# First and last two iterations with their own orders, weights prepared on GpSimd, fusion products in other banks, filler matmuls

## What is computed

```python
q, k, v = (silu(causal_conv4(xn @ W)) for W in (Wq, Wk, Wv))
beta = sigmoid(xn @ Wb)
# delta rule over time; its triangular system is inverted per block
delta = delta_rule(l2norm(q), l2norm(k), v * beta, beta)
# depthwise convolutions of 3, 15 and 31 taps on v, then two products
ms = channel_mixer(kernel_mix(concat(conv3(v), conv15(v), conv31(v))))
feat = concat(xn, mean|ms|, mean|delta|, mean|v|)      # 512 + 12 columns
w = softmax(gelu(feat @ w1 + b1) @ w2 + b2)            # 3 weights per head
o = w0 * ms + w1 * delta + w2 * v
att = (o * rsqrt(mean(o * o)) * o_norm_w) @ Wo
# ffn: mixing of each token with the one before it
ffn = sigmoid(xr @ Wr.T) * ((relu(xk @ Wk.T) ** 2) @ Wv.T)
out = x + att + ffn
```

## Time and profile before

| | us |
|---|---|
| median of 3 runs | 3527.82 (3523.88 to 3529.14) |
| the profiled execution | 3519.07 |
| its span, first to last instruction | 3517.3 |
| TensorE busy | 3315.3 (94%) |
| VectorE busy | 3165.9 (90%) |
| ScalarE busy | 2758.2 (78%) |
| GpSimd busy | 807.7 (23%) |

### The profile page before, as it was taken

The page is one execution under the profiler, slowest core; times in us unless marked ns, Lnnn a source line. Parts: engine busy times, 40 slices in busy tenths (PEclk is TensorE's granted clock), DMA queues, the critical chain, the costliest instruction groups (busy, mean ns, idle before and its releaser), DMA issues.

```text
span 3517.3 us, 69963 instructions
## 1 busy us (share of the span) xinstructions
PE 3315.3 (94%) x22848; PEld 2447.8 (70%) x22848; DVE 3165.9 (90%) x7856; ACT 2758.2 (78%) x9144; POOL 807.7 (23%) x1489
## 2 busy tenths in 40 slices
PE   6899999999999999999999999999999999999986
PEld 5677777667777667776677776777766677767754
DVE  6999998999999999989999999999899899989993
ACT  5677888778887778787778887778877788877774
POOL 2022221122221222221222211222212222112220
PEclk8999999999999999999999999999999999999998
DMA  6022221122211122211222111222111222112220
GB/s 183 11 50 51 50 40 33 29 51 51 50 32 33 37 51 51 50 28 25 49 51 51 36 38 29 50 51 50 32 33 38 51 50 43 35 24 51 45 44 7
DMA packets 188307, 154.92 MB, mean 44 GB/s; under 512 B 111804, under 2 KB 146108, under 8 KB 187688
## 3 DMA queue, kind: packets, MB, share of 16 engines
q0 software_dynamic: 31744, 79.70, 13.1%
q1 hardware_dynamic: 156200, 70.76, 7.7%
HBM read 51.34 MB, written 52.95 MB: 30 GB/s over the span
## 4 chain that ended last, share of the span: by engine, by line
PE 35%; DVE 25%; ACT 21%; issue 9%; DMA 7%; POOL 2%; ACTq 0%; DVEq 0%; POOLq 0%; SPq 0%
DVE my L1531 19%; PE dense L721 6%; DMA my<-prod 5%; PE dense L674 5%; PE dense L678 5%; PE dense L662 3%; ACT my L1106 3%; PE small L690 2%; ACT dense L1136 2%; PE cell L644 2%; PE cell L645 2%; PE cell L637 2%; ACT kT L926 1%; DMA rows_out<-Bm 1%; ACT xsh L856 1%
## 5 line engine op out<-in xcount | busy, mean ns | idle before, releaser
L1531 DVE SCALAR_TENSOR_TENSOR my<-vT,mw,my 128x256 f32<-128x256 f32 x5408 | 2245.4, 480 | 38.9 <-DMA my<-prod 24.3
L721 PE MATMUL dense<-xsh,w 128*128 128x256 f32 x2048 | 483.2, 382 | 3.9
L397 POOL TENSOR_SCALAR vare<-xsq 128x2 f32<-128x2 f32 x32 | 6.2, 194 | 2081.8 <-ACT xsh L856 2081.8
L721 PEld LDWEIGHTS dense<-xsh,w 128*128 128x128 f32 x2048 | 369.4, 190 | 72.3 <-ACT xr L1168 11.1
L1079 ACT ACTIVATE ka<-dense 128x512 f32<-128x512 f32 x64 | 38.2, 597 | 319.3 <-PE dense L662 319.3
L662 PE MATMUL dense<-xk,wfk 128*128 128x256 f32 x1024 | 250.1, 400 | 22.0 <-DVE xb L1591 16.8
L662 PEld LDWEIGHTS dense<-xk,wfk 128*128 128x128 f32 x1024 | 198.4, 199 | 74.9 <-issue 47.0
L674 PE MATMUL dense<-wr,xr 128*128 128x512 f32 x512 | 235.4, 603 | 0.0
L516 PE MATMUL front<-xsh,wq 128*128 128x256 f32 x1024 | 231.9, 379 | 0.0
L678 PE MATMUL dense<-wfv,ka 128*128 128x512 f32 x512 | 230.2, 592 | 0.0
L516 PE MATMUL front<-xsh,wv 128*128 128x256 f32 x1024 | 228.7, 381 | 0.8 <-ACT xsh L871 0.8
(11 more groups left out here) (182 smaller groups left out, 6803.2 us busy)
## 6 DMA issues: line engine op xcount, KB each, us to landing
my<-prod POOLq DMA_DIRECT2D x160, 384.0 KB, 4.2
xa<-in_x SPq DMA_DIRECT2D x32, 512.0 KB, 4.2
rows_out<-Bm SPq DMA_DIRECT2D x64, 256.0 KB, 4.3
out<-xb POOLq DMA_DIRECT2D x32, 512.0 KB, 14.7
Yq<-units_out SPq DMA_DIRECT2D x128, 32.0 KB, 2.1
w<-in_w SPq DMA_DIRECT2D x1, 2048.0 KB, 17.2
Bu<-rows_out SPq DMA_DIRECT2D x32, 64.0 KB, 2.9
units_out<-Xu SPq DMA_DIRECT2D x32, 64.0 KB, 2.5
```

The source lines that it names most:

```text
L721: e.matmul(by_batch(o), w1[:, k, hs(2 * pair + c)], xsh[s % 2][:, k, :, 1:1 + P], start=(k == 0), stop=False)
L1531: i = e.scalar_tensor_tensor(o, vT[s % 2][:, c, :, off:off + P], mw[:, col:col + 1], o, ALU.mult, ALU.add)
```

## The change

(a) The loop runs over `range(2, NS)` only; what the first two and the last two iterations did is written out, with an order of its own on TensorE, ScalarE, VectorE and GpSimd. In the first two, ScalarE sums and squares x of step 1 right after x of step 0, GpSimd takes `deviation(1)` early and `norms_k(0)` and `norms_q(0)` last, and ScalarE copies and starts convolving each projected pair as it comes. In the last two, `ffn_out` of the last step moves ahead of the joining of the block inverse, `state` behind the logits, and `scale_B`, `copy_beta` and others take other places. (b) `prepare_weights` moves from VectorE to GpSimd, behind the inversion of step 0, in 12 instead of 15 instructions: a part is now taken away from the rows below it by a mask that is 1 from row 36 j to the end. (c) In the last step pairs 0 and 1 of `hidden` use the `front` banks, and their product with x (`begin_last_hidden`, 32 matmuls) is issued one iteration earlier; pairs 2 and 3 use the `dense` banks and wait for `ms_done` instead of for gelu. (d) `keep_streaming(s, n)` issues n matmuls of 128 x 512 in float32 into the bank `turn`, which nobody reads: 3 ahead of `turn_features` and 13 behind `turn_logits`, in the last step. The 30 middle iterations keep their instructions and their order, and SyncE's program stays.

```diff
+        def hidden_bank(s, pair):
+            return front[pair] if s == NS - 1 and pair < 2 else dense[pair % 2]
+
...
+            def prepare_weights():
+                done = 0
+
+                def then(ins):
+                    nonlocal done
+                    done += 1
+                    ins.then_inc(scaled, 1)
+                    e.wait_ge(scaled, done)
+
+                e.wait_ge(split_in, 16 * (2 + PARTS * PARTS))
+                whole, taken = (t[0:NROW, :, :].rearrange("p b d -> p (b d)") for t in (ms, dl))
+                for k in range(CB):
+                    then(e.tensor_scalar(wo[:, k, :], wo[:, k, :], onw[:, 0:1], None, ALU.mult))
+                then(e.tensor_copy(ident16[:, :], ident))
+                then(e.tensor_copy(w1x[:, :], whole))
+                for j in range(1, PARTS):
+                    later = cst[0:NROW, C_PART + j:C_PART + j + 1]
+                    then(e.tensor_scalar(taken, w1x[:, :], later, None, ALU.mult))
+                    then(e.tensor_tensor(whole, whole, taken, ALU.subtract))
+                    then(e.tensor_copy(w1x[:, :], whole))
+                assert done == N_SCALED
...
+            deviation(0)
+            deviation(1)
+            clear_units(0)
+            add_taps(0, 2, 0)
+            add_taps(0, 3, 0)
+            invert_units(0, 0, 3)
+            add_taps(0, 3, 1)
+            invert_units(0, 3, 5)
+            invert_units(0, 5, 7)
+            invert_units(0, 7, 9)
+            add_taps(0, 3, 2)
+            invert_units(0, 9, 11)
+            invert_units(0, 11, 13)
+            invert_units(0, 13, 15)
+            add_taps(0, 3, 3)
+            prepare_weights()
+            norms_k(0)
+            norms_q(0)
+            for i in range(2, NS):
+                deviation(i)
...
+            add_taps(NS - 1, 2, 0)
+            add_taps(NS - 1, 3, 0)
+            add_taps(NS - 1, 3, 1)
+            add_taps(NS - 1, 3, 2)
+            invert_o(NS - 2, 0)
+            invert_o(NS - 2, 1)
+            add_taps(NS - 1, 3, 3)
+            clear_units(NS - 1)
+            invert_units(NS - 1, 0, 3)
+            invert_units(NS - 1, 3, 5)
+            invert_units(NS - 1, 5, 7)
+            invert_units(NS - 1, 7, 9)
+            invert_units(NS - 1, 9, 11)
+            invert_units(NS - 1, 11, 13)
+            invert_units(NS - 1, 13, 15)
+            add_out(NS - 2)
+            norms_q(NS - 1)
+            norms_k(NS - 1)
+            invert_o(NS - 1, 0)
+            invert_o(NS - 1, 1)
+            add_out(NS - 1)
...
             def turn_features(s):
                 if s == 0:
                     e.wait_ge(scaled, N_SCALED)
+                if s == NS - 1:
+                    keep_streaming(s, 3)
                 e.wait_ge(*f_low.upto(s))
                 for b in range(NB):
                     e.matmul(s_ft[:, hs(b)], fparts[:, b, :, :, :].rearrange("p j i n -> p (j i n)"), ident16[:, :],
                              start=True, stop=True).then_inc(f_turned.sem, 1)
 
+            def keep_streaming(s, n):
+                e.wait_ge(*tok_done.upto(s))
+                for _ in range(n):
+                    e.matmul(turn[:, :], ident, wo[:, 0, :], start=True, stop=True)
+
+            def begin_last_hidden(s):
+                e.wait_ge(*bq_done.upto(s))
+                e.wait_ge(*raw_done.upto(s))
+                for pair in range(2):
+                    for c in range(2):
+                        for k in range(CB):
+                            e.matmul(by_batch(front[pair][:, c * W:(c + 1) * W]), w1[:, k, hs(2 * pair + c)],
+                                     xsh[s % 2][:, k, :, 1:1 + P], start=(c == 0 and k == 0), stop=False)
+
             def hidden(s, pair):
                 if s == 0:
                     e.wait_ge(fusion_in, 64)
                     e.wait_ge(scaled, N_SCALED)
-                if pair < 2:
-                    e.wait_ge(*ms_done.upto(s, pair))
+                last = s == NS - 1
+                begun = last and pair < 2
+                if pair < 2 or last:
+                    e.wait_ge(*ms_done.upto(s, pair % 2))
                 else:
                     e.wait_ge(*hid_done.upto(s, pair - 2))
                 for c in range(2):
-                    o = dense[pair % 2][:, c * W:(c + 1) * W]
-                    for k in range(CB):
-                        e.matmul(by_batch(o), w1[:, k, hs(2 * pair + c)], xsh[s % 2][:, k, :, 1:1 + P], start=(k == 0),
-                                 stop=False)
+                    o = hidden_bank(s, pair)[:, c * W:(c + 1) * W]
+                    if not begun:
+                        for k in range(CB):
+                            e.matmul(by_batch(o), w1[:, k, hs(2 * pair + c)], xsh[s % 2][:, k, :, 1:1 + P], start=(k == 0),
+                                     stop=False)
                     e.wait_ge(*f_done.upto(s))
-                    i = e.matmul(o, w1x[:, hs(2 * pair + c)], ftT[:, :], start=False, stop=True)
+                    i = e.matmul(o, w1x[:, hs(2 * pair + c)], ftT[:, :], start=False, stop=(c == 1 or not begun))
                 i.then_inc(hid_mm.sem, 1)
 
...
+                if s == NS - 1:
+                    keep_streaming(s, 13)
...
+            turn_beta(NS - 1)
+            begin_last_hidden(NS - 1)
+            query_key(NS - 1, 0)
...
+            ffn_key(NS - 1, 0)
+            ffn_key(NS - 1, 1)
+            ffn_out(NS - 1, 0)
+            inverse_W(NS - 1)
+            turn_tokens(NS - 1, 3)
+            inverse_Z(NS - 1)
+            join_W(NS - 1)
+            join_Z(NS - 1)
+            ffn_out(NS - 1, 1)
+            half_W(NS - 1)
+            half_X(NS - 1)
+            key_state(NS - 1, 0)
+            solve(NS - 1, 1)
+            solve(NS - 1, 0)
+            kernel_mix(NS - 1, 2)
+            outputs(NS - 1, 0)
+            outputs(NS - 1, 1)
+            kernel_mix(NS - 1, 3)
+            channel_mix(NS - 1, 0)
+            channel_mix(NS - 1, 1)
+            turn_features(NS - 1)
+            hidden(NS - 1, 0)
+            hidden(NS - 1, 1)
+            hidden(NS - 1, 2)
+            hidden(NS - 1, 3)
+            logits(NS - 1, 0)
+            logits(NS - 1, 1)
+            turn_logits(NS - 1)
+            state(NS - 1, 0)
+            state(NS - 1, 1)
+            turn_o(NS - 1, 0)
+            turn_o(NS - 1, 1)
+            attend(NS - 1, 0)
+            attend(NS - 1, 1)
...
+            sum_x(0)
+            square_x(0)
+            normalize(0, 0)
+            normalize(0, 1)
+            copy_xnT(0, 0)
+            copy_xnT(0, 1)
+            sum_x(1)
+            square_x(1)
+            copy_raw(0, 0)
+            short_first(0, 0)
+            copy_raw(0, 1)
+            short_first(0, 1)
+            short_silu(0, 0)
+            copy_raw(0, 2)
+            short_silu(0, 1)
+            first_taps(0, 0)
+            first_taps(0, 1)
+            short_first(0, 2)
+            normalize(1, 0)
+            copy_raw(0, 3)
+            short_first(0, 3)
+            normalize(1, 1)
...
+            copy_logits(NS - 2)
+            square_q(NS - 1)
+            exp_logits(NS - 2)
+            first_taps(NS - 1, 2)
+            weigh_delta(NS - 2, 0)
+            weigh_ms(NS - 2, 0)
+            copy_mix(NS - 1, 0)
+            weigh_v(NS - 2, 0)
+            weigh_delta(NS - 2, 1)
+            multiply_taps(NS - 1, 3, 0)
+            first_taps(NS - 1, 3)
+            weigh_v(NS - 2, 1)
+            copy_beta(NS - 1)
+            weigh_ms(NS - 2, 1)
+            tanh_beta(NS - 1)
+            copy_tokens(NS - 1, 1)
+            multiply_taps(NS - 1, 3, 1)
+            mix_half(NS - 1)
+            square_o(NS - 2, 0)
+            multiply_taps(NS - 1, 3, 2)
+            square_o(NS - 2, 1)
+            scale_B(NS - 1, 0)
+            scale_B(NS - 1, 1)
+            normalize_o(NS - 2, 0)
+            multiply_taps(NS - 1, 3, 3)
+            copy_oT(NS - 2, 0)
+            normalize_o(NS - 2, 1)
+            copy_oT(NS - 2, 1)
+            relu_key(NS - 1, 0)
+            square_key(NS - 1, 0)
+            relu_key(NS - 1, 1)
+            square_key(NS - 1, 1)
+            copy_mix(NS - 1, 1)
+            copy_tokens(NS - 1, 2)
+            tanh_gate(NS - 1, 0)
+            copy_W(NS - 1)
+            copy_tokens(NS - 1, 3)
...
-        N_SCALED = CB + 1 + 3 * PARTS + 1
+        N_SCALED = CB + 2 + 3 * (PARTS - 1)
...
-        cst[j * PARTS * NF:(j + 1) * PARTS * NF, C_PART + j] = 1.0
+        cst[j * PARTS * NF:, C_PART + j] = 1.0
```

More of the change, by code:

```diff
@@ new lines, in tensor_program @@
+            kernel_mix(NS - 2, 2)
+            outputs(NS - 2, 0)
+            outputs(NS - 2, 1)
+            ffn_out(NS - 2, 1)
+            state(NS - 2, 0)
+            kernel_mix(NS - 2, 3)
+            state(NS - 2, 1)
+            channel_mix(NS - 2, 0)
+            channel_mix(NS - 2, 1)
+            project(NS - 1, 5)
+            turn_features(NS - 2)
+            hidden(NS - 2, 0)
+            hidden(NS - 2, 1)
```

(20 more changed lines are left out.)

1370 lines of the change are left out of this document (880 added, 490 removed).

## The result

The changed kernel takes 3513.35 us (median of 6 runs, 3509.89 to 3518.19) against 3526.22 (6 runs, 3523.88 to 3529.14) for the kernel before: a ratio of 0.9964, 95% interval 0.9951 to 0.9977, or 12.9 us less (8 to 17 by the interval). Forecast were 3508.8 us and 19 us less: the time lies inside the range, and the kernel is faster, as said, but the gain is two thirds of the forecast's. That the sum came out near does not make its terms right: two were far off, with opposite signs, and the experiments are about those.

The account below looks back on a forecast made before the run. VectorE was taken as late in the first 106 us, a chain through all engines as the bound in the last 65. Start 9.7 plus end 9.4 gave 19 us off 3527.82: 3508.8, range 3496 to 3521.

Parts of the forecast that it names:

- (2): Start: ScalarE handles x of step 1 before copying the first projection; VectorE convolves from 25.6, not 28.67; net 5.2 us.
- (3): Start: nothing else is late; all three chains meet and `step_Y(0)` comes at 89, 17.3 us earlier.
- (1): Start: taking weight preparation off VectorE, all of it in front of `step_Y(0)`, gains 12.5 us.
- (4): Start: GpSimd's 12 weight instructions take 16 us (11 to 22); norms behind them just hidden, 5 us more would show.
- Rival B: Start: GpSimd needs 22 us or more, norms late; start wins 3, not 9.7; 12 in all, 3516; chance 0.17.
- (5): Start: VectorE and GpSimd disturb each other, about 1 ns per GpSimd element; 7 us taken back, bounds 0 and 11.
- (6): Start: TensorE idles about 5 us before the solve, then runs partly at the lower clock; 1 us charged.
- (7): End: `begin_last_hidden` moves 32 matmuls into TensorE's idle time at the wait for `scale_B(31)`; gain 6.2 us.
- (8): End: fillers fit and keep TensorE's clock up; 0.7 us for hidden products, 0.5 for `attend`; bounds 0 and 2.9.
- (9): End: `ffn_out(31, 1)` ahead of the half inversion frees the path from last tap to `channel_mix`; gain 2, bounds -1 and 9.5.
- Rival C: End: `scale_B(31)` moves to about 3402 to 3404, so `Yq` may come late; typically gain 7, 3521; chance 0.18.

Follow-up runs that it names:

- start_only: First two iterations as in the changed kernel, weights on GpSimd, the rest as in the kernel before: 3516.87 us, ratio 0.9978 to the kernel before.
- end_only: Last two iterations, banks and fillers as in the changed kernel, start and weights as in the kernel before: 3522.67 us, ratio 0.9988.
- experiment 4: Changed kernel, weights on ScalarE: 3502.1 us. Its columns: stretch us, busy us (xcount) of TensorE, weight loads, VectorE, ScalarE, GpSimd, then granted clock.
- vector_weights: Changed kernel with its twelve weight operations back on VectorE, ahead of `step_Y(0)`: 3512.2 us, ratio 0.9958 to the kernel before.
- scalar_weights: Changed kernel with weights prepared on ScalarE, two subtractions on VectorE, none on GpSimd: 3502.1 us, ratio 0.995 to the kernel before.
- stream_best: Changed kernel with weights on ScalarE, `ffn_out(31, 1)` cut in two and three filler products in the start's inversion: 3502.71 us, ratio 0.9924.

## Why the prediction was right and where it was wrong

- **(2) and (3), the walk of the start, held.** VectorE began at 25.96 (25.6), waited 2.26 (2) for the first taps, and `step_Y(0)` stood at 91.78 (89, and 1.5 for the port).
- **(1) is hardly a gain of the move.** 12.5 us left the front of `step_Y(0)`, but the new preparation is shorter wherever it runs: on VectorE it took 8.6 (90.58 to 99.20). The medians with it there and on GpSimd can't be told apart; at `step_Y(1)` the move is worth 2 to 5 us. The new order by itself brings VectorE to the preparation 3.3 us earlier (90.58 against 93.86). No run has the new order with the old 15 instructions, so how the rest of the start's gain divides between the order and the shorter preparation is not shown.
- **(4) was too low.** GpSimd took 22.6 us, not 16, just over my upper end: a product of 1024 elements with a scalar 2.89, where memset had suggested 1 to 2. "5 us more would show" was wrong: ScalarE waited for the norms until 105.84, but had to copy the half inverse only at 108.42, when TensorE had finished it (108.38). Rival B's number for the start, 3, did not come, though its condition did.
- **(5) was right in size** (9 to 11 expected, 9.2 seen, 7 booked; the iteration behind `step_Y(0)` is 7.1 longer) **and wrong in form**: not 1 ns for each element, but 0.85 with one input and 2.2 with two.
- **(6) was mis-sized**, 1 instead of 2 to 3.5: only once VectorE was free did the slow clock behind the inversion show (109.5 and 107.9 us for the iteration, then 106.0 with fillers). In the changed kernel the two lie over each other, so it costs little as long as the port is paid. Start in all: 7.4 by its profile, 5.0 by start_only's, 5.8 by the mean of six, 7.8 by start_only's ratio; I had 9.7.
- **(7) held** behind the last tap: 6.2 forecast, 6.1 by the profiles. By the medians leaving it out costs more, 10 us with a wide interval.
- **(8) was mis-sized**: 1.2, with 2.9 as the upper bound; 4.2 by the profiles (2.4 for three, 1.8 for thirteen; 0.6 of the 2.4 lie in `attend`, which differs as much between the kernel before, 8.53, and start_only, 9.08, whose ends are the same). I had counted on low speed returning in the idle stretches around the fillers; it did not. The fillers themselves took twice what I had said, 2.74 and 11.40 us instead of 1.3 to 2 and 5.6 to 8: I had priced one row of the view for each, and each is two. They just fitted.
- **(9) is the term that failed.** The gap between last tap and `channel_mix` did shrink from 3.9 to 2.1, as said, but the last tap moved away: 139.2 behind `step_Y(30)` became 145.1. Of these 5.9 us, 3.8 are idle time of VectorE (8.8 and 12.6); the named waits of the two timelines add to 7.9 and 11.1, where my walk had 8.5. The other 2.1 are busy time, though the operations' own lengths sum to nearly the same (153.6 and 153.9): they overlap less. That successive ones wait for each other more often would explain it; no run shows it. The largest wait, 2.59, is for the way from `step_Y(31)` over two copies and three products to `key_state`, 16.65 us of which the new order covers 14.1 with work; the old one covered 17.5 of 18.2. Term (9) was +2 with -1 as the lower bound; the end's 5.2 less 6.1 and 4.2 makes it -5. Moving all of `ffn_out` does not mend it, and moving its half only shifts the loss behind the last tap.
- **Rival C** came near: B(31) was scaled at 3398.75 and VectorE waited 0.34 and 0.44 us for it around `turn_Y`. Not later, so it took almost nothing.

Not all of the -5 of term (9) is the order's. The six profiles with this order differ by 4.1 us up to the last tap, and by end_only's, the best of them, term (9) is -1.6: a loss all the same. What differs among them is TensorE's clock. In the 20 us behind `step_Y(30)` the changed kernel was granted 0.89 and end_only 1.00, and VectorE had two waits, 0.86 and 1.04 us, that end_only had not. The 10 us behind `step_Y(31)`, of the changed kernel and of end_only (columns as in experiment 4):

```profile
3430.42:3440.42 10.00, 9.08 (x92) 4.95 (x93) 9.89 (x25) 7.80 (x27) 0.00 (x0) 0.67 0.10 43
```

```profile
3435.96:3445.96 10.00, 9.08 (x94) 4.61 (x95) 9.89 (x25) 7.80 (x27) 0.00 (x0) 0.83 0.07 29
```

With 0.67 and 0.68 (vector_weights) the wait ahead of `subtract_state(31, 0)` was 2.59 and 2.49 us; with 0.83 it was 1.72 to 1.78, in four profiles. In the kernel before the same stretch had 1.00 and a wait of 0.67. My walk took its lengths from there. Why the clock differs from one execution to the next is open.

The total was right partly by luck: within the end, (8) came out 3 us better than forecast and (9) 7 worse. A start 2.3 and an end 4.2 too good are small against a range that took in GpSimd at its bound.

## What to carry to other kernels

An operation that was moved to GpSimd was paid for by VectorE's operations with two tensors: price it by its inputs and their elements, not by its length, and look first whether ScalarE idles nearby. When one engine is relieved, ask for the next thing in the same stretch; here it was TensorE's clock, and three products of no use took 2.1 us off a wait. Before a mark is compared between two kernels, look how far it moves between profiles with the same instructions. Of a piece that is moved so that a later one can start sooner, check that the later one's own last input does not move too.

## What the runs showed that was not expected

- GpSimd with a scalar from memory is slower than with two tensors: 1024 elements take 2.89 us as against 2.45 and 2.65 (means over 90: 3.27 and 2.62), a cast 1.04 to 1.11, a memset 0.955. The Trainium skill's "GPSIMD Engine Reference" (section "4.1 Engine selection") calls operations with one input roughly as fast as the line rate; VectorE takes 0.75 for the same product, so this form is not.
- Beside such a product other taps run at full speed (472 ns) and just one is held, for 0.86 us; beside an operation with two inputs of 8 elements none is, though it takes 1.74 us.
- TensorE ran on at a lower granted clock even behind waits of 0.9 to 1.9 us between short products of 32 rows: 0.73 from 91.9 to 101.9 us in scalar_weights, and 1.00 from 92.9 to 102.9 in stream_best, with one product of 512 columns in each wait.
